# Second matrices of eight experts: from two whole buffers to a ring of five half buffers

## What is computed

```
x = x + cross_attention(layernorm(x), ctx)      # 16 heads, 257 context rows per batch
x = x + local_attention(layernorm(x))           # window of 5 rows
h = layernorm(x)
e = argmax(h @ Wr + br)                         # one of 8 experts for each row
x = x + gelu(gelu(h @ W1[e] + b1[e]) @ W2[e] + b2[e]) @ W3[e] + b3[e]
```

## Time and profile before

| | us |
|---|---|
| time, median of 3 runs | 751.25 (750.15 to 752.66) |
| time of the profiled execution | 755.89 |
| span of its trace, first to last instruction | 752.9 |
| TensorE busy | 711.8 (95%) |
| VectorE busy | 469.1 (62%) |
| ScalarE busy | 452.7 (60%) |
| GpSimd busy | 425.5 (57%) |

### The profile page before, as it was taken

One profiled execution on the slowest core, in us unless ns is written; L12 is line 12 of the kernel. 1 busy time (PEld: TensorE's weight loads), 2 busy tenths in 40 slices (PEclk: granted clock), 3 DMA queues, 4 the chain that ended last, 5 costly groups with the idle time before them and its releaser, 6 DMA issues.

```text
span 752.9 us, 26418 instructions
## 1 busy us (share of the span) xinstructions
PE 711.8 (95%) x9203; PEld 604.7 (80%) x9204; DVE 469.1 (62%) x1378; ACT 452.7 (60%) x1071; POOL 425.5 (57%) x564
## 2 busy tenths in 40 slices
PE   8999999999999999999999849998999999997994
PEld 7788888888888888888888737887888788886874
DVE  4466677667766776777767589959625861196000
ACT  4657666666666666666666154756566565654762
POOL 6466656565556555555653114766666667574643
PEclk9999999999999999999999969999999999999997
DMA  7222232333232433243325603274127412360000
GB/s 224 82 74 80 78 92 77 91 70 98 77 91 64 103 77 91 63 103 78 85 73 179 251 14 113 78 248 148 43 79 232 160 36 89 129 213 17 21 7 0
DMA packets 55439, 73.92 MB, mean 98 GB/s; under 512 B 6269, under 2 KB 41118, under 8 KB 55392
## 3 DMA queue, kind: packets, MB, share of 16 engines
q1 hardware_dynamic: 49248, 60.36, 27.5%
q0 software_dynamic: 2944, 8.13, 3.6%
q10 hardware_dynamic: 3200, 4.80, 1.7%
HBM read 66.90 MB, written 7.27 MB: 99 GB/s over the span
## 4 chain that ended last, share of the span: by engine, by line
PE 81%; DVE 10%; DMA 3%; ACT 2%; issue 2%; SPq 0%; POOLq 0%; POOL 0%; ACTq 0%; DVEq 0%
PE ps_s L1684 14%; PE ps_kv L1324 11%; PE ps_kv L1316 10%; PE ps_p L1363 7%; PE ps_s L1335 5%; PE ps_o L1349 5%; DVE w L1298 4%; PE ps_o L1704 3%; DVE w L1295 3%; PE ps_p L1636 3%; PE ps_kv L1636 3%; DMA w_raw<-in_L_ffn_W_dram 3%; PE ps_m L1458 2%; PE ps_m L1415 2%; PE ps_m L1394 2%
## 5 line engine op out<-in xcount | busy, mean ns | idle before, releaser
L766 ACT ACTIVATE prob<-prob,neg_max 128x257 f32<-128x257 f32 x256 | 111.2, 500 | 46.0 <-DVE neg_max L966 44.4
L966 DVE CUSTOM_DVE_ANT_0 prob<-ps_s,mask_add 128x257 f32<-128x257 f32 x256 | 94.8, 422 | 65.1 <-PE ps_s L1335 65.1
L1295 DVE CAST w<-w_raw 128x512 fp32r<-128x512 f32 x94 | 70.2, 747 | 75.8 <-DMA w_raw<-in_L_ffn_W_dram 75.8
L1684 PE MATMUL ps_s<-w,h_hi 128*128 x368 | 93.5, 406 | 12.3 <-DVE w L1298 5.3
L603 POOL TENSOR_TENSOR ctx_parts<-ctx_raw,ctx_parts 128x512 fp32r<-128x512 f32 x64 | 82.7, 1293 | 31.2 <-ACT ctx_parts L761 30.3
L1298 DVE TENSOR_TENSOR w<-w_raw,w 128x512 fp32r<-128x512 f32 x112 | 98.0, 878 | 3.7
L1684 PEld LDWEIGHTS ps_s<-w,h_hi 128*128 128x128 f32 x368 | 68.3, 190 | 31.9 <-issue 17.3
L1316 PE MATMUL ps_kv<-ctx_parts,wkv_hi 128*128 128x256 f32 x512 | 85.9, 295 | 0.2 <-POOL ctx_parts L603 0.2
L1324 PE MATMUL ps_kv<-wkv_hi,ctx_parts 128*128 128x256 f32 x512 | 84.9, 293 | 1.0 <-ACT kT L770 0.7
L1363 PE MATMUL ps_p<-ident,prob 128*128 128x128 f32 x512 | 77.4, 273 | 0.9 <-DVE probT L988 0.8
L706 POOL TENSOR_TENSOR h_lo<-h,h_hi 128x512 fp32r<-128x512 f32 x46 | 64.9, 1412 | 23.4 <-ACT h_hi L884 23.3
(11 more groups left out here) (247 smaller groups left out, 1538.0 us busy)
## 6 DMA issues: line engine op xcount, KB each, us to landing
w_raw<-in_L_ffn_W_dram SPq DMA_DIRECT2D x24, 1024.0 KB, 7.8
ctx_raw<-in_ctx_turned_dram SPq DMA_DIRECT2D x63, 256.0 KB, 3.6
mask_add<-mask_dram SPq DMA_DIRECT2D x64, 128.5 KB, 3.4
rows_dram<-x3n ACTq DMA_DIRECT2D x16, 256.0 KB, 4.3
w_raw<-in_L_ffn_W_dram SPq DMA_DIRECT2D x8, 512.0 KB, 5.6
xt<-in_x_dram SPq DMA_DIRECT2D x16, 128.0 KB, 2.1
xr<-in_x_dram SPq DMA_DIRECT2D x16, 128.0 KB, 2.3
slot_x<-rows_dram,slot_ids POOLq DMA_INDIRECT x23, 3.7
```

Source lines behind the costliest of these rows:

```text
L766: a.activation(prob[:, g, :], prob[:, g, :], ACT.Exp, bias=neg_max[:, g:g + 1], scale=-1.0).then_inc(exp_done, 1)
L966: d.tensor_tensor_reduce(prob[:, r, :], ps_s[r][:, 0:J], mask_add[:, k, :], -(HD ** -0.5), 3.0e38, ALU.add, ALU.min, neg_max[:, r:r + 1]). ...
L1295: d.tensor_copy(w[:, b, HI, part], raw[:, b, part]).then_inc(rounded, 1)
L1684: last = t.matmul(ps_z2[:, :], h1_parts[hp][:, f, :], weight(w23, e % BUFFERS23, wp, f * F2, F2), start=(hp == HI and wp == HI and f == 0) ...
```

## The change

W2 and W3 get buffers apart. A half of W2 has a buffer of its own, and there are five of these, used in turn: half h of expert e is turn 2e+h and lies in place (2e+h) mod 5. W3 keeps two buffers. A half waits for the half five turns before it: half 1 of e still waits for expert e-2, half 0 of e for expert e-3 (half 0 of expert 2 for none). In the order of loads, and of VectorE's rounding, half 0 of e+1 now stands behind W3 of e; after W1 of 2 comes half 0 of 2. Thus LATE is: W1 of 2, half 0 of 2, then for each e from 2: W1 of e+1, half 1 of e, W3 of e, half 0 of e+1. Every late load that has a predecessor in its buffer now reads the slot at which to wait for itself; before, one read served the three pieces of an expert.

`area` grows by 4096 columns (16 KB a partition). To make room, ten tiles of the attention part (`bv_rows`, `band_shifted`, `xt`, `q`, `qd`, `attn_turned`, `attnT`, `x2`, `x2_kept`, `lprob`) are laid by `passing` one behind the other into the HI halves of ring places 1 and 3; as `bv_rows` has 257 columns, those behind it start at odd columns. Attention's weights, and the tables of the routing, lie over other ring places than before. The number of matmuls, of rounding instructions and of bytes loaded stays the same.

```
...
-    COLS1, COLS23 = D // P * F1, F1 // P * F2 + F2 // P * D
-    W3_AT = F1 // P * F2
-    BUFFERS1, BUFFERS23 = 3, 2
+    COLS1, COLS2, COLS3 = D // P * F1, F1 // P * F2 // 2, F2 // P * D
+    BUFFERS1, RING, BUFFERS3 = 3, 5, 2
...
-        sb("area", [P, 2 * (BUFFERS1 * COLS1 + BUFFERS23 * COLS23)])
-        at23 = 2 * BUFFERS1 * COLS1
+        sb("area", [P, 2 * (BUFFERS1 * COLS1 + RING * COLS2 + BUFFERS3 * COLS3)])
+        at2 = 2 * BUFFERS1 * COLS1
+        at3 = at2 + 2 * RING * COLS2
         w1 = over("w1", "area", 0, [P, BUFFERS1, 2, COLS1], F32R)
-        w23 = over("w23", "area", at23, [P, BUFFERS23, 2, COLS23], F32R)
+        w2 = over("w2", "area", at2, [P, RING, 2, COLS2], F32R)
+        w3 = over("w3", "area", at3, [P, BUFFERS3, 2, COLS3], F32R)
 
         w1_raw = over("w1_raw", "area", 0, [P, BUFFERS1, 2, COLS1])[:, :, LO, :]
-        w23_raw = over("w23_raw", "area", at23, [P, BUFFERS23, 2, COLS23])[:, :, LO, :]
+        w2_raw = over("w2_raw", "area", at2, [P, RING, 2, COLS2])[:, :, LO, :]
+        w3_raw = over("w3_raw", "area", at3, [P, BUFFERS3, 2, COLS3])[:, :, LO, :]
 
         def place1(b, part):
             return (2 * b + part) * COLS1
 
-        def place23(b, part):
-            return at23 + (2 * b + part) * COLS23
+        def place2(slot, part):
+            return at2 + (2 * slot + part) * COLS2
+
+        passing_at = {1: 0, 3: 0}
+
+        def passing(name, shape):
+
+            columns = math.prod(shape[1:])
+            slot = min(s for s in passing_at if passing_at[s] + columns <= COLS2)
+            passing_at[slot] += columns
+            return over(name, "area", place2(slot, HI) + passing_at[slot] - columns, shape)
...
-        lw_qk = over("lw_qk", "area", place23(0, HI), [P, 2, D])
-        lw_v = over("lw_v", "area", place23(0, HI) + 2 * D, [P, 2, D + 1])
-        lw_turned = over("lw_turned", "area", place23(0, LO), [P, 2, 2, D])
-        wq = over("wq", "area", place23(0, HI) + 6 * D, [P, 2, D])
+        lw_qk = over("lw_qk", "area", place2(4, HI) + 12 * D, [P, 2, D])
+        lw_v = over("lw_v", "area", place2(0, HI), [P, 2, D + 1])
+        lw_turned = over("lw_turned", "area", place2(0, LO), [P, 2, 2, D])
+        wq = over("wq", "area", place2(4, HI) + 14 * D, [P, 2, D])
...
-        bv_rows = sb("bv_rows", [P, D + 1])
-        band_shifted = sb("band_shifted", [P, P])
+        bv_rows = passing("bv_rows", [P, D + 1])
+        band_shifted = passing("band_shifted", [P, P])
         br_rows = sb("br_rows", [P, E])
-        wkv = over("wkv", "area", place23(0, HI) + 8 * D, [P, 2, 2, D])
-        wkv_hi = over("wkv_hi", "area", place23(0, HI) + 12 * D, [P, 2, 2, D], F32R)
-        wkv_lo = over("wkv_lo", "area", place23(0, HI) + 16 * D, [P, 2, 2, D], F32R)
+        wkv = over("wkv", "area", place2(4, HI), [P, 2, 2, D])
+        wkv_hi = over("wkv_hi", "area", place2(4, HI) + 4 * D, [P, 2, 2, D], F32R)
+        wkv_lo = over("wkv_lo", "area", place2(4, HI) + 8 * D, [P, 2, 2, D], F32R)
...
-        xt = sb("xt", [P, D])
+        xt = passing("xt", [P, D])
...
-        q = sb("q", [P, 2, P])
-        qd = sb("qd", [P, BT, 2, HP * S])
+        q = passing("q", [P, 2, P])
+        qd = passing("qd", [P, BT, 2, HP * S])
...
-        attn_turned = sb("attn_turned", [P, BT, 2, S])
-
-
-        attnT = sb("attnT", [P, 2, P])
+        attn_turned = passing("attn_turned", [P, BT, 2, S])
+
+
+        attnT = passing("attnT", [P, 2, P])
         xr = sb("xr", [P, D])
-        x2 = sb("x2", [P, D])
-        x2_kept = sb("x2_kept", [P, D])
+        x2 = passing("x2", [P, D])
+        x2_kept = passing("x2_kept", [P, D])
...
-        lprob = sb("lprob", [P, P])
+        lprob = passing("lprob", [P, P])
...
-        at_routing = place23(1, HI) + E * D
+        at_routing = place2(2, HI)
...
-        PIECES = (slice(0, W3_AT // 2), slice(W3_AT // 2, W3_AT), slice(W3_AT, COLS23))
-
-        ROUNDED_EARLY = [(0, None), (0, 0), (0, 1), (0, 2), (1, None)]
-        EARLY = [(True, 0), (False, 0), (True, 1), (False, 1)]
-        LATE = [(True, 2)]
+        FIRST, HALVES, THIRD = "w1", ("w2 half 0", "w2 half 1"), "w3"
+        PARTS = {FIRST: (w1, w1_raw, w1_in, BUFFERS1, COLS1), HALVES[0]: (w2, w2_raw, w2_in, RING, COLS2),
+                 HALVES[1]: (w2, w2_raw, w2_in, RING, COLS2), THIRD: (w3, w3_raw, w3_in, BUFFERS3, COLS3)}
+
+        ROUNDED_EARLY = [(FIRST, 0), (HALVES[0], 0), (HALVES[1], 0), (THIRD, 0), (FIRST, 1)]
+        EARLY = [(part, e) for e in range(2) for part in (FIRST,) + HALVES + (THIRD,)]
+        LATE = [(FIRST, 2), (HALVES[0], 2)]
         for e in range(2, E):
-            LATE += [(True, e + 1)] * (e + 1 < E) + [(False, e)]
+            LATE += [(FIRST, e + 1)] * (e + 1 < E) + [(HALVES[1], e), (THIRD, e)] + [(HALVES[0], e + 1)] * (e + 1 < E)
+
+        def turn_of(part, e):
+
+            return 2 * e + HALVES.index(part) if part in HALVES else e
...
+            def load_part(part, e):
+                _, raw, arrived, buffers, _ = PARTS[part]
+                b = turn_of(part, e) % buffers
+                if part == FIRST:
+                    w, n = W1[e], F1
+                elif part == THIRD:
+                    w, n = W3[e], D
                 else:
-                    for piece in range(3):
-                        load_other(e, piece)
+                    half = HALVES.index(part)
+                    w, n = W2[e][half * F1 // 2:(half + 1) * F1 // 2, :], F2
+                sp.dma_start(raw[:, b, :].rearrange("p (k n) -> p k n", n=n), w.rearrange("(k p) n -> p k n", p=P)).then_inc(arrived[b], 16)
...
-            for first_matrix, e in LATE:
-                before = e - (BUFFERS1 if first_matrix else BUFFERS23)
-
-                last_slot = sp.value_load(slot_end_int[0:1, before:before + 1], min_val=1, max_val=SLOTS) if before >= 0 else None
-                if first_matrix:
-                    if before >= 0:
+            for part, e in LATE:
+                buffers = PARTS[part][3]
+                before = turn_of(part, e) - buffers
+                if before >= 0:
+                    other = before // 2 if part in HALVES else before
+                    last_slot = sp.value_load(slot_end_int[0:1, other:other + 1], min_val=1, max_val=SLOTS)
+                    if part == FIRST:
                         sp.wait_ge(z1_filled, 2 * last_slot)
-                    load_first(e)
-                else:
-                    for piece in range(3):
-                        if before >= 0 and piece == 0:
-                            sp.wait_ge(z2_filled, last_slot)
-                        if before >= 0 and piece == 2:
-                            sp.wait_ge(y_filled, last_slot)
-                        load_other(e, piece)
+                    elif part == THIRD:
+                        sp.wait_ge(y_filled, last_slot)
+                    else:
+                        sp.wait_ge(z2_filled, last_slot)
+                load_part(part, e)
...
-            for first_matrix, e in EARLY + LATE:
-                w, raw, buffers, w_in_buffer, ready = ((w1, w1_raw, BUFFERS1, w1_in, w1_ready) if first_matrix else
-                                                      (w23, w23_raw, BUFFERS23, w23_in, w23_ready))
-                b = e % buffers
...
-                        last = d.tensor_tensor(w[:, b, LO, part], raw[:, b, part], f32(w[:, b, HI, part]), ALU.subtract)
-                        if at + 512 == columns.stop:
-                            last.then_inc(ready, 1)
-                        elif early:
-                            last.then_inc(rounded, 1)
-                            k += 1
-                            dve.wait_ge(rounded, k)
+            for matrix, e in EARLY + LATE:
+                w, raw, arrived, buffers, columns = PARTS[matrix]
+                ready = w1_ready if matrix == FIRST else w23_ready
+                b = turn_of(matrix, e) % buffers
+                dve.wait_ge(arrived[b], 16 * (turn_of(matrix, e) // buffers + 1))
+                early = (matrix, e) in ROUNDED_EARLY
...
-                                last = t.matmul(ps_z2[:, :], h1_parts[hp][:, f, :], weight(w23, e % BUFFERS23, wp, f * F2, F2),
+                                last = t.matmul(ps_z2[:, :], h1_parts[hp][:, f, :], weight(w2, (2 * e + half) % RING, wp, f % 4 * F2, F2),
...
-                        last = t.matmul(ps_y[:, 0:D], h2_parts[hp][:, c, :], weight(w23, e % BUFFERS23, wp, W3_AT + c * D, D),
+                        last = t.matmul(ps_y[:, 0:D], h2_parts[hp][:, c, :], weight(w3, e % BUFFERS3, wp, c * D, D),
...
```

More of the change, by code:

```diff
@@ L232, in perceiver_kernel @@
         w1_in = [sem(f"w1_in{i}") for i in range(BUFFERS1)]
-        w23_in = [[sem(f"w23_in{i}_{piece}") for piece in range(3)] for i in range(BUFFERS23)]
+        w2_in = [sem(f"w2_in{i}") for i in range(RING)]
+        w3_in = [sem(f"w3_in{i}") for i in range(BUFFERS3)]
         rounded = sem("rounded")
@@ L495, in _ @@
                 load_x(xr, T, xr_in)
[L497 to L507, removed]
```

(66 more changed lines are left out.)

## The result

The changed kernel takes 747.36 us (median of 7 runs, 745.99 to 749.24) against 751.25. The medians lie 3.9 us apart. The ratio, from runs of both on one chip, is 0.9944 with an interval of 0.9929 to 0.996, or 4.2 us of 751.25. The forecast was 747.0 us, 4.3 us faster. Its profiled execution took 747.56 us, near its median, while that of before was 4.6 us above its own. So the two traces lie further apart (span 752.9 and 745.1) than the two kernels do, and I read stages and periods from them, not spans.

A forecast was written before the change was run, and what follows sets the result against it. TensorE, busy for 95% of the span, was taken as the bound. Waits and low clock gave -6.59 us, the place +2.3, in all -4.3: from 751.25 to 747.0 us, own range 745.5 to 748.5, overall 743.7 to 750.2.

The forecast's parts named there:

- Both waits go: TensorE's layer 2 waits for VectorE's rounding, 1.14 us at slot 4 and 3.87 us at slot 18, would vanish.
- VectorE is done 3.1 us ahead of TensorE: Slot 18: 14 pairs instead of 18, at 1.69 us each, make half 1 of expert 7 ready at 681.4.
- Rival B: Slot 18's wait shrinks but stays, at VectorE's slow pace of 2.03 us a pair: 748.6 to 750.1 us; 18%.
- 1.14 us at slot 4: TensorE's wait in layer 2 for half 1 of expert 2 would go, saving 1.14 us.
- 3.87 + 1.58 at slot 18: Wait for half 1 of expert 7, 3.87 us, and the low clock after it, 1.58 us, would both go.
- The place, +2.3 us: Computing a half's place before layer 2 adds one register instruction, 0.1 us, in all 23: 2.3 us; bounds 0 and 4.6.
- rival A: Computing the place before layer 2 costs nothing, fitting the old instruction: 6.6 us faster, 744.7; 15%.
- SP's reads: Every late load reads its slot itself, two more short reads an expert on SP: costed at nothing.
- the second megabyte at 456: Added load of half 0 of 2 shares DMA engines with slot 2's gather; covered by 2.6 us, costed at nothing.
- attention: Attention's tiles at new, mostly odd columns: costed at nothing, with 1 us allowed for the layout.
- The sequencer as a rival (C): TensorE's sequencer makes the kernel slower, from 0.29 us more in each layer 2; at 0.4 us, 753.9; 9%.
- half 0 one expert earlier: In the load and rounding order, half 0 moves one expert earlier, removing both waits: 1.14 + 3.87 + 1.58 = 6.59 us.

The follow-up runs named there:

- four_old: Changed kernel with four W2 places in use instead of five and the old order of loads; ratio to the kernel before 0.9994.
- wait6: Changed kernel, half 0 of expert 6 loaded directly ahead of half 1 and held until expert 4's last layer 2; ratio to the kernel before 1.0000.
- again: Kernel before, unchanged, run and profiled a second time; ratio 0.9994, span 748.5 us.
- before: The kernel before the change, unchanged; 751.25 us, its profiled execution 755.89 us.
- wait2: Changed kernel, half 0 of expert 2 loaded directly ahead of half 1 and held until expert 0's last layer 2; ratio to the kernel before 0.9942.
- dear2: Changed kernel with layer 2's place computed by more steps to the same value, adding one register instruction; ratio to the kernel before 0.9966.
- late6: Changed kernel, half 0 of expert 6 loaded and rounded behind W1 of 7, directly ahead of half 1, without an added wait; ratio to the kernel before 0.9924.
- hoist: Changed kernel, TensorE's sequencer loading the next slot's expert number ahead of layer 3 in four of five slots; 742.75 us, ratio to the kernel before 0.9894.
- dear3: Changed kernel with layer 2's place computed in eleven steps, in two full register instructions; ratio to the kernel before 1.0004.
- five_old: Changed kernel with its five W2 places but the old order of loads and rounding; ratio to the kernel before 0.9939.

## Why the prediction was right, step by step

**Both waits go: right, and for slot 18 shown.** The changed kernel has no wait for VectorE in two profiled executions, nor has any experiment that keeps its releases. `four_old` and `wait6`, which take the release from half 0 of 6, have the wait of slot 18 again, with the ratio at 1. That of slot 4 is gone too, but `again` and `four_old` lack it without the change, so its going is not shown to be the change's work.

**VectorE is done 3.1 us ahead of TensorE: right.** The 14 pairs were counted rightly. They took 22.7 us (655.76 to 678.47), 1.62 a pair for 1.69, and the slack was 4.3 us. Rival B, at 2.03 a pair, needed one slow piece to be the rule. The slow pairs are those under which GpSimd computes (see the last section), and it does so in part of each slot only.

**1.14 us at slot 4: mis-sized.** The wait belonged to the profiled execution. `again` has none there, `four_old`'s period is 12.18 with the loads in the old order, just that of the change. Of the four traces in which half 0 of 2 waits for expert 0, that of `before` has a period of 13.68, 1.5 us over the changed kernel's, in an execution 4.6 us above its median. `again`, `wait2` and `four_old` have 12.62, 12.60 and 12.18: there the worth is between 0 and 0.4 us.

**3.87 + 1.58 at slot 18: right, 0.3 us too much.** In executions near the median, the period falls from 16.95 and 17.05 (`again`, `four_old`) to 11.85: 5.1 to 5.2 us, for 5.45. That the slow matmuls are part of the wait's price holds in every kernel that has the wait: the granted clock is 0.70 to 0.73 over the 5.5 to 6 us behind it (`before`, `again`, `four_old`, `wait6`), and 1.00 without it.

**The place, +2.3 us: the term that was furthest off.** I took it as one more register instruction in each layer 2. It came to 17 ns a layer, 0.4 us in all: rival A's case, which had 15% (its 744.7 missed as well, since it kept the 6.6 us saved). The estimate of 0.1 us for an instruction more was near, as far as `dear2` shows: 0.11 us for a second one of 32 ns and a first one 36 ns longer. What failed was the step from more operations to more instructions.

So the mechanism of the gain was right, but that 747.0 lies within 0.4 us of the measured 747.36 is luck: it came about from two errors of opposite sign. By what the runs show, with the middle of 0 and 0.4 for slot 4, the sum is -5.1 -0.2 +0.4 = -4.9 us. The three measurements of the changed kernel, 0.9944, 0.9921 and 0.9941, are -4.2, -5.9 and -4.4, mean -4.9. The prediction's -4.3 had 1.3 us too much saved (6.59 for 5.3) and 1.9 too much paid (2.3 for 0.4).

**Costed at nothing, and nothing: SP's reads, the second megabyte at 456, attention.** With a read of its own, half 1 of 6 goes out 1.3 us behind half 0 in `four_old` (647.95 and 649.26), where it was 0.4 in the kernel before; the wait of slot 18 is 3.39 us there and 3.31 in `again`, so the reads cost nothing that can be told. TensorE turned the rows of slot 2 at 467.82 without a wait, so the gather was covered. One wait of 0.4 us for a gather is new, that of slot 0:

```profile
453.75 0.44 PE L1638 MATMUL ps_m<-ident,slot_x 128*128 128x128 f32 x2 [0.38 <-DMA slot_x<-rows_dram,slot_ids]
```

It is over before the added load goes out at 456.9, so this load is not its cause; `late6`, `wait6` and `hoist` have the load and not the wait, and what it comes from stays open. For attention, `four_old` is the evidence. By the Trainium skill (SBUF — State Buffer, "Door 1: The DMA port swizzle") an access that crosses into a new 16-byte line pays a penalty, which would have made ten tiles of attention dearer. No run here shows that: 0.9994 (0.9979 to 1.0009) with all ten moved.

**The sequencer as a rival (C).** Its mechanism is real: `dear3` gives back the whole gain with 0.2 us a slot. Its point of decision, worked out as 0.29 us from 6.59 us saved, lies near 0.23, since the saving is 5.3.

**The new order: not asked, and not needed.** The prediction told the gain as coming from "half 0 one expert earlier". `five_old` has it all with the halves in the old order.

## What to carry to other kernels

A buffer more pays where a load waits for a release that falls just before the engine's busiest stretch: look for the place where two short stages follow a long one, and ask which load could go before them. A wait that the trace shows once may be that execution's own; count on it only if the releases leave it no slack at all, as at slot 18, where VectorE had 18 pairs to do in any execution. And on an engine that is 95% busy, what its sequencer does between two groups of matmuls is on the path: read the times of its instructions from the records instead of counting operations, and move a read of memory to where matmuls are under way.

## What the runs showed of the hardware

- A register instruction of TensorE's sequencer took up the further steps of the place for 15 ns (109 for 94). With more steps it grew to 145 ns and a second one of 32 ns came behind it; then the weight load came 0.11 us later, 2.4 us over 23 layers.
- The sequencer's read of the slot's expert from memory, with the check of its value, costs time when it stands ahead of layer 2. In the changed kernel the check stands between the last weight load of the layer before and the first of layer 2 in 21 of 23 slots in one trace and 17 in the other, in `hoist` in 5. Taking it away from those 12 to 16 gave 3.1 us, 0.19 to 0.26 us each.
- Pairs of the same two instructions on VectorE took from 1.06 us (660.44 to 661.50) to 3.2 (668.58 to 671.76) in one stretch of the changed kernel. The trace names the neighbour: under the long pair GpSimd computes `h_lo` (two subtractions, 668.05 to 671.28), under the short one it only issues a gather. From 470 us on, in both kernels, a CAST of the rounding takes at most 0.62 us and its subtraction at most 0.77 unless a TENSOR_TENSOR of GpSimd is under way at the same time, and up to 1.56 and 1.84 when one is. No run takes GpSimd's work away, so this is a coincidence in time and not a tested cause.
